# q and k as float32r pairs in 48 rows: two score products side by side in the halves of the array, in the maximum phase and in the attention phase

## What is computed

```
q, k, v = split(xn @ Wqkv.T)                       # 16 heads of 16 numbers
dots = where(causal, q @ k.T * 16 ** -0.5, -inf)   # 4 batches x 16 heads x 2048 x 2048
out  = softmax(dots) @ v @ Wout.T + bout
gate, up = fp4_linear(xn, w_gate), fp4_linear(xn, w_up)    # 704 wide, blocks of 16 rounded to fp4
ffn = fp4_linear(silu(gate) * up, w_down)
```

## Time and profile before

| | before |
|---|---|
| median of three runs | 3049.91 us |
| lowest, highest | 3048.52, 3054.88 us |
| profiled execution: span from first to last instruction | 3047.1 us |
| projection (stretch 77 to 230 us) | 153 us, DVE busy 136 us |
| maximum phase (251.5 to 1257 us) | 1005.5 us, PE busy 740 us, DVE 724 us, ACT 638 us |
| attention phase (1281.2 to 3047 us) | 1765.8 us, PE busy 1715 us, ACT 1290 us, DVE 1028 us |

### The profile page before, as it was taken

One profiled execution on the slowest core, in us unless ns is written; L12 is line 12 of the kernel. 1 busy time (PEld: TensorE's weight loads), 2 busy tenths in 40 slices (PEclk: granted clock), 3 DMA queues, 4 the chain that ended last, 5 costly groups with the idle time before them and its releaser, 6 DMA issues.

```text
span 3047.1 us, 60898 instructions
## 1 busy us (share of the span) xinstructions
PE 2621.8 (86%) x18236; PEld 1350.3 (44%) x18236; DVE 1949.4 (64%) x5533; ACT 2030.3 (67%) x3510; POOL 694.1 (23%) x510
## 2 busy tenths in 40 slices
PE   2995777777777777599999999999999999999999
PEld 2872333333333333244444544444544444544445
DVE  6986677776777767455656456665556565555665
ACT  1655566665666666387777577777577777677775
POOL 3652212222122222221121121121122111111121
PEclk9997788887888888799999999999999999999999
DMA  2772211121111121322023122113212203302200
GB/s 74 256 255 59 55 47 50 51 53 53 47 50 50 53 53 48 80 43 43 22 37 75 46 37 47 35 28 66 61 28 42 43 22 63 73 22 38 48 21 31
DMA packets 115564, 175.52 MB, mean 58 GB/s; under 512 B 23344, under 2 KB 91696, under 8 KB 114736
## 3 DMA queue, kind: packets, MB, share of 16 engines
q1 hardware_dynamic: 95856, 147.32, 20.2%
q10 hardware_dynamic: 16576, 15.73, 1.9%
q0 software_dynamic: 2816, 8.91, 1.1%
HBM read 129.37 MB, written 42.53 MB: 56 GB/s over the span
## 4 chain that ended last, share of the span: by engine, by line
PE 49%; ACT 4%; issue 3%; DMA 1%; SPq 1%; DVE 0%; ACTq 0%; POOL 0%; DVEq 0%; POOLq 0%
PE O L925 15%; PE S L909 14%; PE F L945 9%; PE F L985 5%; ACT probs L1054 4%; PE F L975 2%; PE S L996 2%; PE S L912 2%; SPq L528 1%; DMA y<-in_L_attn_x_dram 1%; PE F L938 1%; DMA q_st<-s_shift 0%; ACTq L1049 0%; DVE o_turned L1260 0%; DVE ht_lo L1248 0%
## 5 line engine op out<-in xcount | busy, mean ns | idle before, releaser
L1054 ACT ACTIVATE probs<-S 128x1024 f32<-128x1024 f32 (+3 forms) x1280 | 1075.1, 897 | 215.6 <-PE S L909 78.0
L751 DVE CUSTOM_DVE_ANT_0 m_excess<-m_S,m_excess 128x512 f32<-128x512 f32 (+7 forms) x1536 | 718.0, 531 | 285.5 <-PE m_S L686 217.3
L730 ACT ACTIVATE m_excess<-m_DIFF 128x512 f32<-128x512 f32 (+7 forms) x1536 | 635.5, 477 | 367.4 <-PE m_DIFF L686 256.1
L684 PE MATMUL m_DIFF<-m_k,m_q_diff 128*128 128x512 bf16 (+7 forms) x1536 | 540.1, 360 | 269.4 <-DMA m_k<-s_k 242.4
L909 PE MATMUL S<-q_st,k_st 128*128 128x512 bf16 (+3 forms) x2560 | 648.4, 351 | 66.1 <-DMA q_st<-s_shift 28.8
L925 PE MATMUL O<-probs,v_sb 128*32 128x512 f32 (+3 forms) x5120 | 603.3, 543 | 2.1 <-POOL v_sb L1131 2.1
L684 PE MATMUL m_S<-m_k,m_q 128*128 128x512 bf16 (+7 forms) x1536 | 539.7, 363 | 6.0 <-DVE m_second_max L751 2.0
L639 POOL TENSOR_TENSOR m_q_diff<-m_zero,m_q 48x2048 bf16<-48x2048 bf16 x64 | 230.4, 3599 | 763.9 <-DMA m_q<-s_q 755.6
L909 PEld LDWEIGHTS S<-q_st,k_st 128*128 128x128 bf16 x2560 | 213.5, 98 | 409.6 <-ACT probs L1054 236.0
L684 PEld LDWEIGHTS m_DIFF<-m_k,m_q_diff 128*128 128x128 bf16 x1536 | 169.9, 111 | 381.4 <-issue 324.9
L684 PEld LDWEIGHTS m_S<-m_k,m_q 128*128 128x128 bf16 x1536 | 165.3, 108 | 168.9 <-DVE m_row_max L751 126.7
(11 more groups left out here) (163 smaller groups left out, 4130.7 us busy)
## 6 DMA issues: line engine op xcount, KB each, us to landing
k_st<-s_k SPq DMA_DIRECT2D x96, 256.0 KB, 8.7
q_st<-s_q SPq DMA_DIRECT2D x384, 64.0 KB
s_q<-a_part SPq DMA_DIRECT2D x48, 256.0 KB, 3.0
s_k<-a_part SPq DMA_DIRECT2D x48, 256.0 KB, 2.2
a_x<-in_L_attn_x_dram POOLq DMA_DIRECT2D x16, 512.0 KB, 4.8
s_v<-a_v SPq DMA_DIRECT2D x16, 512.0 KB, 2.9
m_q<-s_q SPq DMA_DIRECT2D x64, 128.0 KB
m_q_diff<-s_q SPq DMA_DIRECT2D x64, 128.0 KB
```

What stands on the lines that cost most here:

```text
L684: ins = pe.matmul(out[:, 0:keys], q[:, i * P:(i + 1) * P], of, start=True, stop=mask is None)
L730: act.activation(excess[u % MAX_EXCESS][:, 0:keys // 2], DIFF[u % MAX_BUFS][:, 0:keys // 2], ACT.Relu) \
L751: dve.tensor_tensor_reduce(larger, S[u % MAX_BUFS][:, 0:keys // 2], larger, 1.0, -3e38, ALU.add, ALU.max, column).then_inc(reduced[u % MAX ...
L1054: act.activation(probs[half][st.n % 2][:, :, 0:st.width], S[half][:, :, 0:st.width], ACT.Exp, scale=SCALE).then_inc(exped[half], 1)
```

## The change

Numbers are now float32r (a float32 with a shortened mantissa) in two parts, high and low, where there were three bf16 parts. Three part products make a score (high high, high low, low high), so a stack has 48 rows, and with two rows of shift 50: it fits in one half of the 128 rows.

- Projection: ACT writes the high parts of q and k, DVE the low parts. POOL makes the difference of the second and the first keys of each pair (three additions or subtractions a group), ACT and DVE split it in `kd_hi` and `kd_lo`, and a new tensor `s_kd` holds it. All parts are stored as 4 bytes.
- Maximum phase: rows 0 to 63 hold q and k, rows 64 to 127 hold q and `kd`. The score product uses the first 64 rows and the difference product the other 64. A unit is a whole query block (up to 1024 columns, in pieces of up to 512), so a head has 16 units; `m_S` and `m_DIFF` have two buffers of two banks each, `m_excess` four. Every load brings two heads, in twelve DMAs. POOL's negation and the joining of two maxima are gone.
- Attention phase: heads 0 and 2 of a group lie in rows 0 to 63, heads 1 and 3 in rows 64 to 127, each in its half of the array. A half step issues its two score products and, on the diagonal, both masks behind them. The masks are bf16 over all 128 rows, as before.

```diff
-PARTS = 3
-STACK = 6 * DH
+PARTS = 2
+STACK = 3 * DH
+ROWS = P // 2
+PAIR = P // 2
...
-        part = [two(f"a_part{k}_", [P, 4, GRP], BF16) for k in range(PARTS)]
-        rest = two("a_rest", [P, 4, GRP])
+        hi = two("a_hi", [P, 4, GRP], F32R)
+        lo = two("a_lo", [P, 4, GRP], F32R)
+        kd_hi, kd_lo = two("a_kd_hi", [P, KD, GRP // 2], F32R), two("a_kd_lo", [P, KD, GRP // 2], F32R)
...
+                pool.tensor_tensor(blocks(diff), *halves(hi), ALU.subtract).then_inc(diff_part, 1)
+                pool.wait_ge(lo_done[1][p], r + 1 + PRIMED)
+                pool.tensor_tensor(blocks(diff_lo), *halves(lo), ALU.subtract).then_inc(diff_part, 1)
+                pool.wait_ge(diff_part, g * 2 + 2 + PRIMED)
+                pool.tensor_tensor(diff[:, :, :], diff[:, :, :], diff_lo[:, :, :], ALU.add).then_inc(diff_done[p], 1)
...
-Q_STACK, K_STACK = (0, 1, 2, 0, 1, 0), (0, 0, 0, 1, 1, 2)
+Q_STACK, K_STACK = (0, 0, 1), (0, 1, 0)
...
-MAX_KEYS = 1024
-MAX_BUFS = 4
-MAX_EXCESS = 8
-MAX_LEAD = 2
+MAX_KEYS = 2048
+MAX_BUFS = 2
+MAX_EXCESS = 4
 MAX_HEADS = 8
+MAX_LOAD = 2
+BANK = 512
...
+    order = [i for n in range(NKB // 2) for i in (NKB - 1 - n, n)]
+    return [(h, i) for h in range(MAX_HEADS) for i in order]
...
+            for p in range(2):
+                sp.wait_ge(zeroed[p], 2)
...
+                    sp.wait_ge(stack_free[p], b * (rounds * loads // 2) + load // 2 + PRIMED)
+
+                    for rows, k_name, tokens in ((slice(0, ROWS), "k", T), (slice(ROWS, P), "kd", T // 2)):
+                        load_stack(sp, k_st[p][rows, :, 0:tokens], dram[k_name][:, load * MAX_LOAD * DH:(load + 1) * MAX_LOAD * DH, :],
+                                   K_STACK, 0, 1, bass.ds(b * tokens, tokens), stack_ld[p])
+                        load_stack(sp, q_st[p][rows, :, :], dram["q"][:, load * MAX_LOAD * DH:(load + 1) * MAX_LOAD * DH, :],
+                                   Q_STACK, 0, 1, bass.ds(b * T, T), stack_ld[p])
...
+            def step(n, ahead, u):
+
+                if ahead is not None:
+                    h = units[ahead][0]
+                    if ahead % per_load == 0:
+                        pe.wait_ge(stack_ld[h // MAX_LOAD % 2], loads_before(n, h // MAX_LOAD) * (16 * load_dmas) + 16 * load_dmas + PRIMED)
+                    pe.wait_ge(exceeded[ahead % MAX_BUFS], uses(n, ahead - MAX_BUFS, MAX_BUFS) + PRIMED)
+                if u is not None:
+                    last = u - MAX_BUFS
+                    pe.wait_ge(reduced[last % MAX_EXCESS], uses(n, last, MAX_EXCESS) + PRIMED)
...
+                for k in range(max(len(parts), len(scores))):
+                    if k < len(parts):
+                        difference(ahead, *parts[k])
+                    if k < len(scores):
+                        score(u, *scores[k])
+                if ahead is not None:
+                    mask(DIFF, ahead, PAIR).then_inc(differed[ahead % MAX_BUFS], 1)
+                if u is not None:
+                    mask(S, u, 0).then_inc(scored[u % MAX_BUFS], 1)
...
-                for s in (2 * half, 2 * half + 1):
-                    ins = pe.matmul(S[half][:, s % 2, 0:st.width], k_st[p][:, s, st.j * P:(st.j + 1) * P],
-                                    q_st[st.c % 2][:, s, st.skip:QC], start=True, stop=not st.diagonal)
-                    if st.diagonal:
-                        ins = pe.matmul(S[half][:, s % 2, 0:P], ident_bf[:, :], future[:, :], start=False, stop=True)
+                for e in range(2):
+                    rows = slice(e * ROWS, (e + 1) * ROWS)
+                    ins = pe.matmul(S[half][:, e, 0:st.width], k_st[p][rows, half, st.j * P:(st.j + 1) * P],
+                                    q_st[st.c % 2][rows, half, st.skip:QC], start=True, stop=not st.diagonal)
+                if st.diagonal:
+                    for e in range(2):
+                        ins = pe.matmul(S[half][:, e, 0:P], ident_bf[:, :], future[:, :], start=False, stop=True)
...
-            pool.memset(k_st[1][STACK:P, :, :].bitcast(F32), TWO_ONES).then_inc(k_ones[1], 1)
+            pool.memset(k_st[1][:, :, :].bitcast(F32), 1.0).then_inc(k_ones[1], 1)
```

More of the change, by code:

```diff
@@ L438, in body @@
                 pe.wait_ge(xt_lo_done[p], r + 1 + PRIMED)
[L440 to L441 removed]
+                for h in (1, 0):
+                    pe.wait_ge(lo_done[h][before[1]], before[0] + 1 + PRIMED)
                     for o in (2 * h, 2 * h + 1):
@@ L605, in shift_phase, with loads_before @@
         aside = once("m_aside")
         rounds = H // MAX_HEADS
-        per_round = MAX_HEADS // 2
-        head_dmas = len(MAX_Q) + 2 * len(MAX_K)
+        loads = MAX_HEADS // MAX_LOAD
+        load_dmas = 4 * STACK_DMAS
         prime(nc, primed)
         block = ctx.enter_context(nc.Block())
-        def heads_before(n, h):
-            return n * per_round + h // 2
-        round_units = [(h, *unit) for h in range(MAX_HEADS) for unit in units]
+        def loads_before(n, load):
+            return n * (loads // 2) + load // 2
@@ new lines, in difference, with mask @@
+            def difference(u, at, width):
+                h, i = units[u]
+                p, s = h // MAX_LOAD % 2, h % MAX_LOAD
+                return pe.matmul(DIFF[u % MAX_BUFS][:, at:at + width], q_st[p][ROWS:P, s, i * P:(i + 1) * P],
+                                 k_st[p][ROWS:P, s, at:at + width], start=True, stop=at + width < (i + 1) * PAIR)
+            def mask(out, u, first):
+                width = (units[u][1] + 1) * PAIR
+                return pe.matmul(out[u % MAX_BUFS][:, width - PAIR:width], ident_bf[:, :], future[:, first:first + PAIR],
+                                 start=False, stop=True)
@@ L721, in _ @@
+            pe.wait_ge(consts, 4)
+            with pe.Fori(0, B * rounds) as n:
+                step(n, 0, None)
+                for u in range(len(units)):
+                    step(n, u + 1 if u + 1 < len(units) else None, u)
+                for buf in range(MAX_EXCESS):
+                    pe.wait_ge(reduced[buf], uses(n, len(units) - 1, MAX_EXCESS) + PRIMED)
+                pe.transpose(turn, row_max[:, :, :].rearrange("p h i -> p (h i)"), ident[:, :]).then_inc(turned, 1)
         @block.scalar
```

285 lines of the change are left out of this document (111 added, 174 removed).

## The result

| | before | after |
|---|---|---|
| median of four runs | 3049.22 us | 3522.12 us |
| lowest, highest | 3047.41, 3054.88 us | 3516.40, 3527.95 us |
| ratio (95% interval) | | 1.1543 (1.1525 to 1.1561) |
| profiled execution, span | 3047.1 us | 3514.8 us |

A forecast was written before the change was run, and what follows sets the result against it. TensorE was taken to bound attention; VectorE's reductions plus a load stall the maximum phase. Attention +95, maximum phase +40 and projection +10 on 3047.1 gave a span of 3192, about 3195 us; range 2860 to 3360.

The forecast's parts named there:

- columns at 0.42 ns (0.215 for 512): Maximum phase: column price in a wide unit's cycle of 0.81 + 1.47 ns x w, giving 15.9 us a head.
- Lower clock or narrow pieces: Rival, chance 0.10: TensorE at 1.2 GHz throughout the maximum phase adds 256 us, 3450 us; narrow float32 products some 30 us.
- the joining of two maxima and a shorter round end: Maximum phase: these two savings together were to take 7 us off.
- The chain over two buffers: Maximum phase: wide scores wait for the buffer just freed, VectorE waits for them; 15.9 us a head against 15.5, +26 us.
- Halves overlap: Both phases: products in the two row halves run side by side; the opposite was a rival, 0.10, 3345 us.
- The second weight load at 0.11: Both phases: the second half's float32r weight load comes 0.11 us behind the first; a full step's scores take 0.85.
- The price of a change of use: Both phases: changing the array's use costs 0.10 us before bf16 weights, 0.21 before float32r weights.
- Diagonal steps: Attention phase: masks between halves lengthen these steps by 0.39 to 0.72 us after a gated operation; 132 us lost.
- Full steps: Attention phase: scores take 0.85 us instead of 0.97; 0.12 saved after a gated operation, 0.10 after O, 43 us gained.
- Loads and starts: Memsets and first loads: +21 us before the maximum phase, +6 before attention, projection +10; later loads of two heads hidden.
- a free change of use: Rival, chance 0.34: changing the array's use costs nothing, so both phases get faster; 2751 us by its sum, 2900 taken.

The follow-up runs named there:

- e1: Changed kernel with the maximum phase's score and difference products over all 128 rows, in series (output not the reference's): 3390 us, maximum phase 1268 us.
- e2: Changed kernel with the maximum phase's score and difference products both in rows 0 to 63, in series: 3698 us, maximum phase 1577 us.
- e4: Kernel before with products and masks of the maximum phase over rows 0 to 63 alone (bf16, four buffers): 3141 us, maximum phase 1095 us.
- e13: Kernel before with load DMAs of 16 rows, plus maximum-phase scores over rows 64 to 127 alone: 8133 us once, then 3453.76 us (ratio 1.1309).
- e7: Changed kernel with units of at most 1024 keys, four buffers and full-row products in series, maxima not joined: 3027 us, maximum phase 907 us.
- e10: Changed kernel with both score products of an attention half step in rows 0 to 63: 3733 us, attention phase 2024 us.
- e8: Changed kernel with a diagonal attention step's masks issued behind both halves' scores: 3473.7 us, attention phase 1766 us.
- e11: Changed kernel without the masks of the attention phase (output not the reference's): 3413 us, attention phase 1702 us.
- e3: Changed kernel without the causal masks in the maximum phase: 3406 us, maximum phase 1283 us.
- e9: Changed kernel with 1024-key units, four buffers, full-row products (zeros in half of q's rows), maxima joined, attention masks last: 3002.24 us, ratio 0.9826.

## Why the prediction was wrong

**The step that failed** is in the maximum phase: "columns at 0.42 ns (0.215 for 512)". That row is from the attention phase, at full clock, and I carried it into a phase whose clock I had not argued. The runs showed the phase at 1.2 GHz throughout, a column at twice the price. My rival "Lower clock or narrow pieces" named the low clock, with a chance of 0.10 and 3450 us, and 3522 was measured; it gave no reason for it, and that half rows bring it (e1, e2, e4, e13) stands nowhere in the prediction. The low clock lengthens more than the columns: a float32r weight load takes 0.28 us, was priced at 0.21 with the change, and 960 columns with their load take 1.1 us. A head is 20.76 us instead of 15.9: 64 x 4.9 = 311 us. A second term failed in the same phase: I had subtracted 7 us for the joining of two maxima and a shorter round end, and the seven turns between rounds grew by some 55 us instead. 311 + 55 + 7 make up, to rounding, the 372 us by which the phase lies above its forecast.

**The chain over two buffers** was seen rightly and is a true cost, 361 us at clocks of 0.83 and 0.89 (e1 against e7). How much of the forecast 1025 us it would take with halves at full clock no run could show, since halves never had that clock in this phase.

**Halves overlap**: right (e2, e10). **The second weight load at 0.11**: wrong, both start together; a full step's scores take 0.76, not 0.85. The row behind that term was misread: two products of 256 columns that start 0.11 apart show the time of 256 columns (256 x 0.42 ns = 0.11 us) and say nothing of a load. **The price of a change of use**: near enough. A half step's pair and its masks take 0.65 us (2661.59 to 2662.24), and the 0.74 priced for them without the second load is 0.63; e13 shows the change between bf16 products.

**Diagonal steps**: right in kind, too dear. 1.30, 1.18, 1.06 and 0.95 us for 512, 384, 256 and 128 columns, against 1.58, 1.47, 1.37 and 1.26. The losses are 0.11, 0.21, 0.30 and 0.41 where I had 0.39 to 0.72. Masks last (e8) give 41 us back, as much as the phase had lost. Full steps gain 0.21 on TensorE behind the gated layer, 252 x 0.21 = 53 us, diagonal steps lose up to 256 x 0.26 = 66; that is +13, and +41.5 were measured. The 31 us more that TensorE waits for ScalarE's exponentials fit the other 28: part of what the full steps gain is waited away where ScalarE sets the pace. No run isolates this.

**Loads and starts**: +27.9 against +31, +7.3 against +6, right, and in their parts too: the projection takes 159 us against 153 (+10 forecast), the stretch to the first product 43.4 against 21.5 (+21 forecast). No load holds up a head.

**The rival on the other side**, a free change of use, did not hold: masks with their changes cost 105 us of the attention phase (e11) and 114 of the maximum phase (e3), and no version with halves in the maximum phase came below the kernel before.

## What to carry to other kernels

Before packing small products into halves of the array, ask what the clock will do: in the maximum phase half-row products kept TensorE at 1.2 GHz even between full-row ones, in the attention phase they did not. Zeros in the unused rows (one more operand tile) kept the granted clock at 0.88, at the price that the products run one after the other. Where two limits are close, undo both before judging either. And look first at the number of DMA engines that a load uses: regrouping its rows gave 8.8%, more than any rearrangement of the products.

## What the runs showed of the hardware

- Products over 64 of 128 rows had a granted clock 0.50 in the maximum phase of nine kernels (float32r and bf16, one half or two, with and without full-row masks, and with the differences over full rows), with TensorE up to 98% busy. With all products over 128 rows it was 0.83 to 0.96, also where half the rows hold zeros (e9).
- The attention phase has half-row scores too and stayed at 0.99, with values and gated-layer products around them; with both heads in one half (e10) its mean was 0.97. What separates the two phases is open.
- Two halves' weight loads start together; two pairs of 512-column products take 0.66 us, the same four in one half 1.14.
- A change between half-row float32r scores and full-row bf16 masks: masks start 0.43 us after the start of a pair of 512 columns, whose columns alone are 0.215, and the next pair 0.22 after the masks. Two changes less shorten a diagonal step of 384 columns by 0.31 us (e8). Between bf16 products at 1.2 GHz a change costs some 0.13 us (e13 against e4).
- At a turn between two rounds of the maximum phase VectorE stood idle for 5.9 to 10.6 us with its inputs ready; the profile shows no releaser.
- One execution ran at a fraction of TensorE's speed with a granted clock of 1.00 in the records (8133 against 3454 us): the granted clock alone doesn't prove full speed.
